# Attention scores packed by four heads into row groups of 32, one signal for the values, a power as root seed, and an input copy moved one tile

## The reference

```python
h = z + _attention(_rmsnorm(z, ln1_w), wq, wk, wv, wo)   # 16 heads of 8 features, softmax over 1024 keys
h = h + _moe(_rmsnorm(h, ln2_w), gate_w, w1, w2, w3)     # top 2 of 8 experts, 256 hidden features
```

## Time and profile before

| | us |
|---|---|
| median of 3 runs | 1236.47 |
| the runs | 1229.24, 1236.47, 1237.98 |
| the profiled execution, its time | 1228.6 |
| its span, first to last instruction | 1226.8 |
| TensorE busy in the span | 1005.9 (82%) |
| VectorE busy | 836.2 (68%) |
| ScalarE busy | 666.3 (54%) |
| GpSimd busy | 418.3 (34%) |

### The profile page before, as it was taken

How to read it: one execution, slowest core, us unless ns; L and a number is a source line. 1 busy time by engine, 2 the same in 40 slices (tenths; PEclk the granted TensorE clock), 3 DMA queues, 4 the chain that set the end, 5 groups by cost and what they waited for, 6 DMA issues and landing times. The chain is left out here.

```text
span 1226.8 us, 21943 instructions
## 1 busy us (share of the span) xinstructions
PE 1005.9 (82%) x5592; PEld 472.9 (39%) x5592; DVE 836.2 (68%) x1286; ACT 666.3 (54%) x1382; POOL 418.3 (34%) x767
## 2 busy tenths in 40 slices
PE   0156666999999999999999999999999968777850
PEld 0034442333333344344344344434443235554530
DVE  5667658789888778888888888888884013232552
ACT  1001111577777677777777777777776534333320
POOL 6103310010110143433433523524522434644576
PEclk9978776899999989999999999999998579988985
DMA  8954566010100110100101101101100012212342
GB/s 269 383 190 137 137 172 172 1 36 10 36 26 10 37 28 10 44 25 20 43 11 33 43 10 35 43 10 35 44 1 2 17 36 64 73 50 70 96 130 71
DMA packets 61944, 81.56 MB, mean 66 GB/s; under 512 B 8512, under 2 KB 39488, under 8 KB 61504
## 3 DMA queue, kind: packets, MB, share of 16 engines
q1 hardware_dynamic: 45808, 51.93, 14.8%
q10 hardware_dynamic: 11984, 20.59, 4.6%
q0 software_dynamic: 4096, 8.40, 2.3%
HBM read 32.12 MB, written 48.23 MB: 65 GB/s over the span
## 5 line engine op out<-in xcount | busy, mean ns | idle before, releaser
L1084 DVE TENSOR_REDUCE smax<-ps 128x2 f32<-128x1024 f32 x512 | 601.7, 1220 | 96.7 <-PE ps L1273 93.5
L853 ACT ACTIVATE prob<-ps 128x512 f32<-128x512 f32 x1024 | 528.8, 603 | 160.2 <-PE ps L1322 157.5
L1322 PE MATMUL ps<-qpack,kpack 34*128 34x512 f32 x1024 | 383.8, 458 | 23.6 <-ACT prob L853 11.7
L1273 PE MATMUL ps<-kpack,qpack 34*128 34x512 f32 x1024 | 314.2, 452 | 10.0 <-DVE smax L1084 9.3
L1322 PEld LDWEIGHTS ps<-qpack,kpack 34*128 34x128 f32 x1024 | 172.9, 189 | 297.2 <-ACT prob L853 250.2
L1332 PE MATMUL ps<-prob,vpad 128*32 128x512 f32 x2048 | 284.7, 629 | 0.0
L1273 PEld LDWEIGHTS ps<-kpack,qpack 34*128 34x128 f32 x1024 | 138.3, 189 | 41.3 <-DVE smax L1084 28.5
L450 POOL MEMSET qpack<- 2x2048 f32 x32 | 57.6, 1799 | 207.9 <-PE ps L1322 205.2
L1190 DVE TENSOR_TENSOR prob<-ps,prob 128x256 f32<-128x256 f32 x80 | 33.9, 424 | 104.9 <-ACT prob L906 104.0
L1498 PE MATMUL ps<-w,ws 128*128 x160 | 89.1, 642 | 15.3 <-ACT ws L899 14.5
L906 ACT ACTIVATE prob<-ps 128x256 f32<-128x256 f32 x80 | 30.8, 385 | 86.3 <-PE ps L1498 86.3
(11 more groups left out here) (211 smaller groups left out, 881.4 us busy)
## 6 DMA issues: line engine op xcount, KB each, us to landing
by_expert_rows<-prob ACTq DMA_DIRECT2D x4, 4864.0 KB, 30.9
q_parts<-qk SPq DMA_DIRECT2D x32, 256.0 KB, 3.8
k_parts<-qk SPq DMA_DIRECT2D x32, 256.0 KB, 4.0
kpack<-k_parts SPq DMA_DIRECT2D x32, 256.0 KB, 3.9
qpack<-q_parts SPq DMA_DIRECT2D x64, 128.0 KB, 3.3
vall<-by_expert_rows SPq DMA_DIRECT2D x80, 64.0 KB, 1.8
by_expert_rows<-vall SPq DMA_DIRECT2D x80, 64.0 KB
w<-w_t SPq DMA_DIRECT2D x3, 1024.0 KB, 10.1
```

The source lines that it names most:

```text
L853: act.activation(prob[:, v % RING, :], bank(col_bank(pos, kind)), ACT.Exp).then_inc(col_free, 1)
L1084: dve.tensor_reduce(smax[:, half, :, pair, qt, kh], ps[:, first:first + 2, :], AX_X, ALU.max).then_inc(row_free, 1)
L1273: ins = pe.matmul(bank(first + par), qpack[r:r + ROWS, slot, half, pair, qt * P:(qt + 1) * P], kpack[r:r + ROWS, slot, pair, kh * HALF:(kh ...
L1322: pe.matmul(bank(col_bank(pos, kind)), kpack[r:r + ROWS, slot, head // 2, kt * P:(kt + 1) * P], qpack[r:r + ROWS, slot, half, head // 2, : ...
```

## The change

- Each of the four heads of a quad gets a row group of 32 partitions (`LANE`): 24 rows for three of the four products of parts (rest times rest is dropped), two rows for the maximum, six unused. Column scores contract 26 rows, row scores the 24 without the maximum; so nothing is cleared any more, and `clear_maxima`, q_clear and its waits are gone. The weights of q and k keep their natural order.
- The pairs of row scores take heads 2 and 3 (partitions 64 and 96) first and heads 0 and 1 second, each beside column scores of heads 0 and 1, then 2 and 3.
- Stored parts: the rest is stored once, not twice. A pack is loaded with one DMA for each head, 12 for a pack instead of 6. The maxima are placed with two DMAs of four separate partitions each.
- `weigh_values` increments pv_done once, by four, on the last matmul.
- GpSimd computes the seed of the root itself as a power with exponent -0.5 (`power`), and does two Newton rounds. The seeds on VectorE and the two semaphores are gone, and VectorE's attention quads are one loop.
- ScalarE's `save_x` is issued after tile 2 of a group instead of tile 3.

```diff
-CROSS = PARTS * PARTS * HD
+TERMS = 3
+CROSS = TERMS * HD
 ROWS = CROSS + PARTS
-ODD = 64
+LANE = 32
...
-        qpack = sb("qpack", [P, 2, 2, HQ // 2, HALF], F32R)
-        kpack = sb("kpack", [P, 2, HQ // 2, L], F32R)
+        qpack = sb("qpack", [P, 2, 2, HALF], F32R)
+        kpack = sb("kpack", [P, 2, L], F32R)
...
+        power = sb("power", [P, 4])
...
-        PACK = 16 * 6
+        PACK = 16 * 3 * HQ
...
-        LATE_SEED = {12: 6, 31: 7}
...
+                            rows = dram[bass.ds(b * (NQ * TERMS * LANE) + j * (TERMS * LANE), TERMS * LANE), :]
+                            whole = qk2[LANE * j:LANE * j + LANE, w, part, :].bitcast(F32)
+                            if part == 0:
+                                both = (0, 2, 1) if w == 0 else (0, 3, 2)
+                                sp.dma_start(rows.rearrange("(o r) l -> r o l", o=TERMS)[:, both[0]:both[1]:both[2], :],
+                                             whole.unsqueeze(1).to_broadcast([LANE, 2, L])).then_inc(parts_out, 16)
                             else:
+                                o = 2 if w == 0 else 1
+                                sp.dma_start(rows[o * LANE:o * LANE + LANE, :], whole).then_inc(parts_out, 16)
...
             def load_k(n, slot):
 
-                for par in range(2):
...
+                for h in range(HQ):
+                    sp.dma_start(kpack[LANE * h:LANE * h + CROSS, slot, :].bitcast(F32),
+                                 of_head(k_parts, n, h)).then_inc(pack_in[slot], 16)
...
             def place_maxima(slot, half):
 
-                for par in range(2):
-                    r = par * ODD + CROSS
-                    sp.dma_start(
-                        qpack[r:r + PARTS, slot, half, :, :].rearrange("p a q -> p (a q)").bitcast(F32),
-                        mtr[16 * par:16 * par + 16, :]).then_inc(m_placed, 16)
+                for part in range(PARTS):
+                    sp.dma_start(qpack[CROSS + part:P:LANE, slot, half, :].bitcast(F32),
+                                 mtr[16 * part:16 * part + 16, :]).then_inc(m_placed, 16)
...
             sp.wait_ge(parts_out, (B - 1) * BATCH_PARTS)
+            sp.wait_ge(pads, 1)
...
+            gp.memset(power[:, :], -0.5).then_inc(consts, 1)
...
-            def clear_maxima(slot):
...
-            clear_maxima(0)
-            clear_maxima(1)
+            gp.memset(kpack[:, :, :].bitcast(F32), 1.0).then_inc(pads, 1)
...
             def refill(i, slot, base, kind):
 
-                gp.wait_ge(col_full, base + (col_pos(UNITS - 1, kind) + 1))
-                gp.wait_ge(vpad_in, 2 * i + (2 + slot))
+                gp.wait_ge(pv_done, i * (2 * UNITS) + ((slot + 1) * UNITS + RING))
                 gp.sem_inc(passed, 1)
-                clear_maxima(slot)
-                gp.wait_ge(q_clear, 4 * i + (2 * slot + 6))
-                gp.wait_ge(pv_done, i * (2 * UNITS) + ((slot + 1) * UNITS + RING))
...
-                gp.tensor_scalar(var, rstd, 1.0 / H, EPS, ALU.mult, ALU.add).then_inc(f_mean, 1)
+                step(gp.tensor_scalar(var, rstd, 1.0 / H, EPS, ALU.mult, ALU.add))
+                step(gp.tensor_tensor(rstd, var, power[:, :], ALU.pow))
...
-                gp.wait_ge(f_seed, t + 1)
-                for _ in range(3):
+                for _ in range(2):
...
-                if j % 4 == 3 and j + 1 < TILES_T:
+                if j % 4 == 2 and j + 2 < TILES_T:
                     save_x(j // 4 + 1)
...
-                    half, pair, qt, kh = p // 16, p % 16 // 8, p % 8 // 2, p % 2
+                    half, pair, qt, kh = p // 16, 1 - p % 2, p % 16 // 4, p % 4 // 2
...
-            def seed(t, before):
...
-                for par in range(2):
-                    r = par * ODD
-                    ins = pe.matmul(bank(first + par), qpack[r:r + ROWS, slot, half, pair, qt * P:(qt + 1) * P],
-                                    kpack[r:r + ROWS, slot, pair, kh * HALF:(kh + 1) * HALF], start=True, stop=True)
+                for n in range(2):
+                    r = (2 * pair + n) * LANE
+                    ins = pe.matmul(bank(first + n), qpack[r:r + CROSS, slot, half, qt * P:(qt + 1) * P],
+                                    kpack[r:r + CROSS, slot, kh * HALF:(kh + 1) * HALF], start=True, stop=True)
...
-                    r = head % 2 * ODD
+                    r = head * LANE
...
-                              start=(kt == 0), stop=(kt == TILES - 1), skip_group_check=True).then_inc(pv_done, 1)
+                    ins = pe.matmul(ps[32 * head:32 * head + VW, PV_BANK, :], vpad[:, slot, kt, head, :],
+                                    prob[:, v % RING, :],
+                                    start=(kt == 0), stop=(kt == TILES - 1), skip_group_check=True)
+                ins.then_inc(pv_done, HQ)
...
-                    pe.wait_ge(q_clear, 2 * quad + 4)
```

More of the change, by code:

```diff
@@ new lines, in of_head @@
+            def of_head(dram, n, h):
+                return (dram[bass.ds(n * (TERMS * LANE), TERMS * LANE), :]
+                        .rearrange("(o h d) l -> h o d l", o=TERMS, h=HQ)[h])
+            def load_k(n, slot):
+                for h in range(HQ):
+                    sp.dma_start(kpack[LANE * h:LANE * h + CROSS, slot, :].bitcast(F32),
+                                 of_head(k_parts, n, h)).then_inc(pack_in[slot], 16)
+            def load_q(n, slot, half):
+                for h in range(HQ):
+                    sp.dma_start(qpack[LANE * h:LANE * h + CROSS, slot, half, :].bitcast(F32),
+                                 of_head(q_parts, n, h)[:, :, half * HALF:(half + 1) * HALF]).then_inc(pack_in[slot], 16)
@@ L1143, in _, with dve_quad @@
             start += 2
-            def dve_quad(i, slot, own, last=False, t=None):
+            def dve_quad(i, slot, own, last=False):
                 base = i * (2 * ROW_ITEMS) + slot * ROW_ITEMS
@@ L1156, in dve_quad @@
                     split_maxima(0, following + (pair_pos(15) + 1), own + 3)
-                    maxima(16, 20, following)
-                    if t is not None:
-                        seed(t, own + 5)
-                    maxima(20, PAIRS - 2, following)
-                    finish_o(quad, 1, following + (O_LATE + 1), row_banks(O_LATE), own + (5 + extra))
+                    maxima(16, PAIRS - 2, following)
+                    finish_o(quad, 1, following + (O_LATE + 1), row_banks(O_LATE), own + 5)
                 else:
@@ L1165, in dve_quad @@
                     finish_o(quad, 1, O_LAST + 2, FINAL_BANK, own + 3)
-            with loop(dve, 0, 2) as i:
+            with loop(dve, 0, QUADS // 2 - 1) as i:
                 own = i * (2 * PER_QUAD) + start
@@ L1170, in _ @@
                 dve_quad(i, 1, own + PER_QUAD)
[L1171 to L1179 removed]
+            start += (QUADS - 2) * PER_QUAD
+            dve_quad(QUADS // 2 - 1, 0, start)
+            start += PER_QUAD
             dve_quad(QUADS // 2 - 1, 1, start, last=True)
@@ L1213, in _ @@
                     save_ht(j - 1)
-                if j in LATE_SEED:
-                    seed(LATE_SEED[j], start)
-                    start += 1
                 if j >= COMBINE and (j - COMBINE) % 4 != 3:
```

94 lines of the change are left out of this document (22 added, 72 removed).

## The result

The changed kernel takes 1492.4 us (median of 4 runs, 1460.3 to 1522.5), the kernel before 1232.9 us on the same chip: a ratio of 1.191, 95% interval 1.181 to 1.201. The executions of a kernel fall into shorter and longer ones by their granted clock (here 1460.3, 1470.3, 1474.3 and 1514.5, 1522.5, 1525.4 us): every ratio and interval in this document compares the shorter ones alone, the times given are medians of all, and the profiled execution of the changed kernel (1522.5 us, span 1520.7) is a longer one. The forecast was 1229.6 us with a range to 1272; the result is slower by 260 us and outside the range.

A forecast was written before the change was run, and what follows sets the result against it. Attention was taken as bound by the 2.70 us score-exp-weighing loop, the late stage by GpSimd. 1228.6 + 0.5 - 6.1 - 1.3 = 1221.7, plus 7.9 to the runs' median gave 1229.6 us; range 1206 to 1272.

The forecast's parts named there:

- the loop of 2.70 us: Attention group: first column score, exp, signal, fourth column score and weighing set the period; row scores are not in it.
- 24 rows instead of 34 ... so nothing: Score matmuls in attention: time goes with the 512 columns, not the rows, so fewer rows change nothing.
- rival A: Attention: the clock falls more often, slower; 1266 us with falls in five odd quads, 1595 throughout; chance 0.25, 0.08 far above.
- "T", four row groups abreast: Attention scores: two slots instead of four, but the fourth column score still waits for the first exp; gain 0.
- rival D: Attention: four row groups do not run abreast and hold the fourth column score, up to +107 us; chance 0.03.
- One signal: 0: Weighing in attention: one increment instead of four leaves the switch to the scores as costly; 0 us.
- Rival B: End of the weighing gets shorter with one increment, 20 to 23 us less, 1208 us; chance 0.12.
- DMAs: +0.5: Pack loads before attention: 12 issues on SyncE instead of 6, mostly covered; +0.5 us, bounds 0 and +2.
- Input copy: -6.1: Expert tiles: issuing save_x one tile earlier removes a 0.81 us wait per group where tiles set the pace; -6.1 us.
- Power: -1.3: GpSimd's root in block 7: seed wait and one Newton round go, a power taken as 0.4 us comes in; -1.3 us.
- rival C: Late stage: the power is slow or the copy delays gate and product, so late gains go; 1237 us; chance 0.10.
- block 6's seed (tile 12) is hidden behind tile 14: Expert stage: removing VectorE's seed wait for block 6 was taken to gain nothing.

The follow-up runs named there:

- two lanes: The kernel before with three products (24 and 26 rows), heads still at partitions 0 and 64, two matmuls abreast: 1501.4 us where the kernel before took 1351.7.
- the best version: The kernel before padded with zero rows from 34 to 64, with the late edits and single signal: 1253.4 us (0.933), in the last set 1208.2 us (0.975).

## Why the prediction was wrong, point by point

**What bounds the kernel, and the loop of 2.70 us: right.** In the changed kernel the group at full clock is still 2.69 us with the score at 1.26 behind the exp. Running the row scores in two slots instead of four gave nothing, as the earlier trace rows said. One reading was off without effect: by the earlier trace rows the second pair of row scores ended at 1.19 before, not at 0.95.

**"24 rows instead of 34 ... so nothing": the step that failed.** For the length of a matmul it is right: 0.50 us with 26, 34 and 64 rows. For the clock it is wrong, and that is 1062 - 756 = 306 us of attention in the profiled execution and 1001.5 - 756 = 245.5 in the shorter one, where the sum had 0. It came back as rival A, with the right effect (the clock), the right rows and even a price, 1595 us for all groups at 4.16. A gave two reasons, fewer rows and a shorter time that the array streams; the runs bear out the first (30 and 32 rows in the same four row groups) and not the second (two lanes lose as much). What was wrong was the argument against it, "the products still run in every group", and with it the chance of 0.08 for A at large. I took the activity of TensorE as matmuls issued; the runs show that rows fed count. The trace of before held the hint: in the last quad the same column scores and weighings went on, the four row scores of a group were gone, and the clock fell within some microseconds (the last row score starts at 933.5, the clock stands at 0.50 in 940 to 944). There 136 rows of 272 were no longer fed (4 matmuls of 34 instead of 8); the change takes 72 of 272 away in every group (4 x 26 + 4 x 24 = 200). To price A from this, the question was whether the kernel stands near the edge; the one fall at 424 to 436 and the spread of its runs are hints that it does, no more, and where the edge lies no run shows.

**"T", four row groups abreast: 0.** Right; rival D did not come (all four start within 0.01 us), and the group of 2.69 us leaves nothing for a gain by the shorter array path.

**One signal: 0.** Right for plain groups; 0.08 us in two groups of 16 went, 2.6 us in all by reckoning, which no time shows. Rival B fell.

**DMAs: +0.5.** The twelve issues took 9.5 us in SyncE's queue, where 8.2 were reckoned, but they began 6.5 us earlier, and attention's first matmul started at 187.97, before at 188.99: -1.0 rather than +0.5. Two traces of one kernel differ by as much (187.97 and 188.86 for the changed one), so it is 0 as far as it can be told.

**Input copy: -6.1, about right.** The step of four tiles went from 7.70 to 6.71, 0.99 rather than 0.81; why by more than the wait is not shown. The first three steps gave 3.2 us, what was forecast for four turns up to the late logits. Up to the copy of the last token block GpSimd was 8.4 us earlier counted from the last weighing: these 3.2, 1.7 by which the first tile itself stood earlier, and 3.4 of the step from tile 12 to 16, which come only with the power. Then TensorE waited at tile 33 (12.46 us; I had some 11). At the end the gathers started 11.1 us earlier, forecast 7; what is left for the turns behind the copy of the block is 2.2, forecast 2.9.

**Power: -1.3, mis-sized.** Two things were off. The power took 1.05 us; I chose 0.4 between 0.20 and 1.04, and the upper end was right: a two-operand power of 128x4 costs what a multiply of 128x512 costs. In block 7 the way from the seed to the scaled rows is 4.91 us, before 5.42: -0.5. That is in rival C's direction, but small. And "block 6's seed (tile 12) is hidden behind tile 14" was wrong: GpSimd had waited 6.8 us for that seed, and without it the step from tile 12 to 16 is 3.4 us shorter. Together some -3.9 (an estimate from these two).

The stage behind attention gained 11 us in both traces of the changed kernel (243.4 to 232.3 and 232.5), and 7.7 in the best version (235.7), where 7.4 was forecast. The profiled execution of the best version is 20 us shorter than that of the kernel before: these 7.7, 11.4 in attention and 1.1 ahead of it. The medians differ by 31 us, 1208 beside 1240; that the other 11 are falls of the clock in the usual execution of the kernel before (mean clock 0.90 there, 0.914 in the one profiled) is likely, but no trace of such an execution was kept.

## What to carry to other kernels

Before rows are taken out of a matmul that TensorE repeats for hundreds of microseconds, look whether the clock falls anywhere in the trace where it is fed less; if it does, fewer rows can cost more than the work they save. A spread of some per cent between runs, and single stretches at 0.50 in the clock row, hint that a kernel stands near such an edge, and padding with zero rows is then an edit to try: it lengthened no matmul here. An edit that takes nothing off the loop that sets the period saves nothing, whatever the engine's busy share is.

## What the runs showed that I had not expected

- Zero rows count for the clock: in one set 34, 48 and 64 rows gave mean clocks of 0.83, 0.90 and 0.92, with one count of matmuls and one length of them at full clock. Rows a group do not order all kernels, though: the four row groups at 30 and 32 (248 a group) stood at 0.84, the two lanes at 34 (272) at 0.83. What else enters is open.
- The same kernel has levels 100 us and more apart (1233 and 1240 us against 1338 to 1369), and they go with a pause that costs some 6 us in every second quad from the sixth on, and with a longer expert stage. The best version lost 45 us between the levels (1208.2 and 1253.4), the kernel before 98 to 129 (1239.7, and 1338.1 to 1369.1); in the latter half clock follows the pause.
- A power on GpSimd takes 1.05 us for 128x4, five times a multiply of that size (0.20).
- A seed of two short instructions on VectorE held GpSimd for 6.8 us, as it stood behind tile 12 in VectorE's order.
